# Graph attention layer on one core: the value product of a unit in two halves behind later scores, and operand stacks filled by halves of the tokens

## What is computed

```python
h = jnp.maximum(_layernorm(x), 0.0)            # x: (8, 1024, 256) f32
q = (h @ Wq + bq).reshape(b, n, 8, 32)         # k and v likewise
scores = jnp.einsum('bqhd,bkhd->bhqk', q, k) / sqrt(32)
scores = scores + (1.0 - adj)[None, None] * -1e9
attn = softmax(scores, axis=-1)
out = jnp.einsum('bhqk,bkhd->bqhd', attn, v).reshape(b, n, 256)
result = x + (out @ Wo + bo)
```

## Time and profile before

| | us |
|---|---|
| median of three runs (1271.64 to 1273.63) | 1272.16 |
| the profiled execution | 1269.52 |
| its span | 1267.7 |
| TensorE busy in the span | 1170.4 (92%) |
| DVE busy | 987.3 (78%) |
| ACT busy | 993.3 (78%) |
| POOL busy | 131.6 (10%) |

### The profile page before, as it was taken

How to read it: one execution, slowest core, us unless ns; L and a number is a source line. 1 busy time by engine, 2 the same in 40 slices (tenths; PEclk the granted TensorE clock), 3 DMA queues, 4 the chain that set the end, 5 groups by cost and what they waited for, 6 DMA issues and landing times.

```text
span 1267.7 us, 30114 instructions
## 1 busy us (share of the span) xinstructions
PE 1170.4 (92%) x10752; PEld 885.5 (70%) x10752; DVE 987.3 (78%) x1802; ACT 993.3 (78%) x1827; POOL 131.6 (10%) x235
## 2 busy tenths in 40 slices
PE   4799999999989999899999999999998999999897
PEld 4576776777767776676766777767776767777665
DVE  4697786977878877887878877888777978778775
ACT  2588886887878977788877878778877888778885
POOL 4002000020001101021010210002000020000001
PEclk9799999999999999999999999999999999999999
DMA  8442061511505134051431515225061320615001
GB/s 278 112 94 75 18 151 36 120 49 40 140 25 134 35 68 117 19 134 35 96 89 27 127 35 127 61 56 124 5 150 53 71 64 1 163 39 113 22 2 51
DMA packets 53470, 100.06 MB, mean 79 GB/s; under 512 B 10032, under 2 KB 35888, under 8 KB 53296
## 3 DMA queue, kind: packets, MB, share of 16 engines
q1 hardware_dynamic: 52720, 96.25, 30.3%
q0 software_dynamic: 576, 1.57, 0.5%
HBM read 22.28 MB, written 8.39 MB: 24 GB/s over the span
## 4 chain that ended last, share of the span: by engine, by line
PE 62%; ACT 21%; issue 8%; DVE 6%; SPq 1%; DMA 1%; ACTq 0%; POOL 0%; DVEq 0%; POOLq 0%
PE ps_turn L681 18%; PE ps_heads L737 18%; PE ps_scores L667 12%; ACT rows L420 11%; ACT turned_p L427 6%; PE ps_side L688 4%; PE ps_side L697 4%; PE ps_side L716 4%; DVE turned_p L515 3%; ACT turned_p L433 2%; SPq L248 1%; DVE rows L504 1%; ACT ht L445 1%; PE ps_turn L688 1%; DVE stats L539 1%
## 5 line engine op out<-in xcount | busy, mean ns | idle before, releaser
L504 DVE CUSTOM_DVE_ANT_0 rows<-ps_scores,mask 128x1024 f32<-128x1024 f32 x512 | 623.2, 1218 | 49.8 <-issue 29.8
L420 ACT ACTIVATE rows<-rows,row_min 128x1024 f32<-128x1024 f32 x512 | 591.5, 1155 | 31.3 <-DVE row_min L504 16.0
L681 PE MATMUL ps_turn<-ident_r,rows_raw 128*128 128x128 f32 x4096 | 499.6, 258 | 53.4 <-DVE turned_p L515 23.9
L681 PEld LDWEIGHTS ps_turn<-ident_r,rows_raw 128*128 128x128 f32 x4096 | 407.7, 141 | 189.2 <-issue 88.2
L427 ACT ACTIVATE turned_p<-ps_turn 128x512 f32<-128x512 f32 x512 | 307.5, 601 | 193.3 <-PE ps_turn L681 191.8
L515 DVE COPY turned_p<-ps_turn 128x512 f32<-128x512 f32 x384 | 263.3, 686 | 173.4 <-PE ps_turn L681 171.6
L667 PE MATMUL ps_scores<-k_stack,q_stack 128*128 128x512 f32 x1024 | 360.9, 434 | 12.3 <-DMA k_stack<-k_lo 12.3
L737 PE MATMUL ps_heads<-turned_p,v 128*32 128x256 f32 x4096 | 247.4, 382 | 11.3 <-ACT turned_p L427 10.8
L737 PEld LDWEIGHTS ps_heads<-turned_p,v 128*32 128x32 f32 x4096 | 120.1, 109 | 107.4 <-ACT turned_p L427 33.7
L667 PEld LDWEIGHTS ps_scores<-k_stack,q_stack 128*128 128x128 f32 x1024 | 153.9, 190 | 14.6 <-issue 7.7
L397 POOL COPY inv_wide<-row_inv 128x256 f32<-128x256 f32 x64 | 25.5, 398 | 1054.1 <-DVE row_inv L551 956.4
(11 more groups left out here) (55 smaller groups left out, 463.3 us busy)
## 6 DMA issues: line engine op xcount, KB each, us to landing
k_stack<-k_hi SPq DMA_DIRECT2D x128, 128.0 KB, 2.4
k_stack<-k_lo SPq DMA_DIRECT2D x128, 128.0 KB, 2.4
q_stack<-q_lo SPq DMA_DIRECT2D x124, 128.0 KB, 2.4
q_stack<-q_hi SPq DMA_DIRECT2D x120, 128.0 KB, 2.4
res<-in_x SPq DMA_DIRECT2D x32, 256.0 KB, 2.7
out<-res SPq DMA_DIRECT2D x32, 256.0 KB, 2.2
xn<-in_x SPq DMA_DIRECT2D x7, 1024.0 KB, 6.1
mask<-in_adj SPq DMA_DIRECT2D x1, 3584.0 KB, 14.8
```

Source lines behind the costliest of these rows:

```text
L420: nc.scalar.activation(rows[:, m % RING, :], rows[:, m % RING, :], ACT.Exp, bias=row_min[:, m % RING:m % RING + 1], scale=-1.0, accum_out= ...
L504: nc.vector.tensor_tensor_reduce(out=rows[:, m % RING, :], in0=ps_scores[m % 2][:], in1=mask[:, qt, :], scale=1.0, scalar=START_MIN, op0=A ...
L681: tr = nc.tensor.transpose(bank[:, k, :].bitcast(F32R), rows_raw[:, i % RING, kt * P:(kt + 1) * P], ident_r[:])
```

## The change

- The value product of a unit is split by key tiles. Half a runs behind the scores in slot 0 of the next unit, half b behind those in slot 3 (`PV_ROW`). The copies of half a and half b go to arrays of their own, turned_a and turned_b, with a place for each row (`place`), doubled for rows 0 (half a) and 0 to 3 (half b), so that the copies of the next unit's first rows don't overwrite what is still to be read. A matmul of it now reads two blocks of 128 columns.
- The row sums are inverted in slot 7 of their own unit, spread and transposed at the end of slot 7, and copied by ACT first in the next slot 0.
- ACT takes the high part, the ht copy and the copy of the inverses ahead of the exponential of its slot; before they stood behind it.
- `STEPS` puts the side work into other slots.
- q's and k's high and low parts hold half of the tokens only. After every qk step SP fills that half of the stack, by 16 transfers of 64 KB. So the high part of step 2 waits until the transfers of steps 0 and 1 have landed.
- Moments come one tile per slot, in slots 10 to 17 of phase 0. POOL normalises in unit 1 and not 2.
- bv isn't added to v any more: at the start TensorE multiplies bv by Wo and DVE adds it to bo.
- HEAD is 10.

```diff
-SIDE_STEPS = (
-    (("qk", 0, (1, 1, 2, 2)), ("o", 3, (3, 3, 4, 4)), ("qk", 1, (5, 5, 7, 7)), ("qk", 2, (9, 9, 11, 11)),
-     ("qk", 3, (13, 13, 14, 14)), ("v", 0, (17, 18, 19, 19)), ("v", 1, (21, 21, 22, 22)),
-     ("ht", 0, (26, 26, 26, 26)), ("ht", 1, (27, 27, 27, 27)), ("ht", 2, (29, 29, 29, 29)),
-     ("ht", 3, (30, 30, 30, 30))),
...
+PV_ROW = (0, 3)
+INV_ROW, NORM_ROW = 7, 4
+PLACES = (1 + UNIT_ROWS, PARTS + UNIT_ROWS)
...
+def place(half, u, r):
+
+    if half == 0:
+        return u % 2 if r == 0 else r + 1
+    return 2 * r + u % 2 if r < PARTS else PARTS + r
...
+STEPS = (
+    (("qk", 0, (1, 1, 2, 2)), ("o", 3, (5, 6, 7, 7)), ("qk", 1, (9, 9, 10, 10)), ("qk", 2, (12, 13, 14, 15)),
+     ("qk", 3, (17, 17, 18, 18)), ("v", 0, (20, 20, 21, 21)), ("v", 1, (23, 23, 25, 25)),
+     ("ht", 0, (27, 27, 27, 27)), ("ht", 1, (28, 28, 28, 28)), ("ht", 2, (29, 29, 29, 29)),
      ("ht", 3, (30, 30, 30, 30))),
...
+    (("qk", 0, (1, 1, 2, 2)), ("v", 0, (4, 4, 5, 5)), ("qk", 1, (6, 6, 7, 7)), ("v", 1, (9, 9, 10, 10)),
+     ("o", 0, (13, 14, 15, 15)), ("qk", 2, (17, 17, 18, 18)), ("qk", 3, (20, 21, 22, 22)),
+     ("o", 1, (25, 25, 26, 26)), ("o", 2, (29, 29, 30, 30))),
 )
```

SP:

```diff
+        def stack_step(eng, g, s):
+            n, cols = "qk"[s % 2], slice(s // 2 * BANK, (s // 2 + 1) * BANK)
+            dst, parts = {"q": q_stack, "k": k_stack}[n][g], parts_of(n, *hi, *lo)
+            for h in range(PARTS):
+                for r in range(PARTS):
+                    eng.dma_start(dst[r * HEAD_DIM:(r + 1) * HEAD_DIM, h, cols].bitcast(F32),
+                                  parts[r][h * HEAD_DIM:(h + 1) * HEAD_DIM, :].bitcast(F32)
+                                  ).then_inc(stacked[g][h], 16)
...
+            def stack(bg, g, s):
+                wait(lo_done, qk_step(bg, g, s) + 1)
+                stack_step(sp, g, s)
...
             def body(b, left):
-                stack(b, 1, row(b, 0, 0) + 1)
+                for s in range(1, QK_STEPS):
+                    stack(b, 1, s)
                 if left > 1:
...
                 if left > 0:
-                    stack(b + 1, 0, row(b, 1, 0))
...
+                    wait(scores_done, row(b, 1, 0) + 1)
+                    stack(b + 1, 0, 0)
+                    stack(b + 1, 0, 1)
+                store(b, 0, True)
+                if left > 0:
+                    stack(b + 1, 0, 2)
+                    stack(b + 1, 0, 3)
+                store(b, 1, True)
+                store(b, 2, left > 0)
+                if left > 0:
+                    first_step(b + 1)
+                store(b, 3, left > 0)
```

ACT's and DVE's slots:

```diff
             def slot(b, g, i, first, last):
+                r = i % UNIT_ROWS
+                kind, s, pieces = side_work(g, i - 1, first, last)
+                done = PIECES - 1 in pieces
+                if kind == "ht" and done:
+                    copy_ht(b + 1, s)
+                if kind == "qk" and done:
+                    nb, ng = next_phase(b, g)
+
+                    for h in range(PARTS):
+                        if s == 0:
+                            act.wait_ge(stacked[g][h], stack_count(g, b + 1))
+                        elif s == 2:
+                            act.wait_ge(stacked[ng][h], stack_count(ng, nb, 2))
+                    high_part(nb, ng, s, hi[s % 2][:])
+                if r == 0 and not (first and i == 0):
+                    copy_inv(unit(b, g, i // UNIT_ROWS) - 1)
                 m = ahead(g, i, EXP_AHEAD)
                 if not (last and m >= BATCH_ROWS):
                     exp(m, row(b, 0, m))
...
+                if r == INV_ROW:
+                    invert(b, g, u, first)
+                if r not in ACT_COPIES:
                     copy_b(b, g, i)
+                if r == NORM_ROW and not first:
+                    norm_heads(unit(b, g, u) - 1, *((g, u - 1) if u else (1 - g, UNITS - 1)))
+                if g == 0 and i in STATS and not last:
+                    moments(b + 1, STATS[i])
```

TensorE:

```diff
-                for kt in range(half * PARTS, (half + 1) * PARTS):
+                for kt in range(PARTS):
                     for h in range(PARTS):
-                        mm = nc.tensor.matmul(ps_heads[h * HEAD_DIM:(h + 1) * HEAD_DIM, 0:UNIT_Q],
-                                              v[g][:, kt, h * HEAD_DIM:(h + 1) * HEAD_DIM],
-                                              turned_p[:, h, kt, :], start=(kt == 0), stop=(kt == TILES - 1))
+                        p0, p1 = place(half, parity, h), place(half, parity, PARTS + h)
+                        mm = nc.tensor.matmul(ps_heads[h * HEAD_DIM:(h + 1) * HEAD_DIM, 0:UNIT_Q]
+                                              .rearrange("p (t n) -> p t n", n=P),
+                                              v[g][:, half * PARTS + kt, h * HEAD_DIM:(h + 1) * HEAD_DIM],
+                                              turned[half][:, p0:p1 + 1:p1 - p0, kt, :],
+                                              start=(half == 0 and kt == 0), stop=(half == 1 and kt == PARTS - 1))
...
             def slot(b, g, i, first, last):
-                n, u = row(b, g, i), i // UNIT_ROWS
-                for half in range(2):
-                    if i % UNIT_ROWS == 0 and not (first and i == 0):
-                        heads(n, unit(b, g, u), g if u else 1 - g, half)
-                    turn(b, g, i, half)
+                u, r = i // UNIT_ROWS, i % UNIT_ROWS
+                turn(b, g, i, 0)
+                turn(b, g, i, 1)
...
+                if r in PV_ROW and not (first and i < UNIT_ROWS):
+                    heads(unit(b, g, u) - 1, u + 1, g if u else 1 - g, PV_ROW.index(r))
...
+                if r == INV_ROW:
+                    turn_inv(b, g, u, first)
```

More of the change, by code:

```diff
@@ L262, in load_res, with wait @@
                              ).then_inc(res_in[u % 2], 16)
[L264 to L271 removed]
+            def wait(done, count):
+                count = held(sp, count)
+                sp.wait_ge(lo_done, QK_STEPS)
+                sp.wait_ge(done, count)
@@ new lines, in _, with spread, unit_work @@
+                stack_start(pool, start_stacked[h], h, "q", range(POOL_COPIES))
+            pool.wait_ge(bo_ready, 1)
+            def spread(b, g, u):
+                count = held(pool, unit(b, g, u) + 1)
+                own()
+                pool.wait_ge(inv_done, count)
+                pool.wait_ge(inv_turned, count)
+                pool.tensor_copy(inv_wide[:], row_inv[:].unsqueeze(2).to_broadcast([P, UNIT_ROWS, HEAD_DIM])
+                                 ).then_inc(inv_spread, 1)
+            def unit_work(b, g, u, last):
+                spread(b, g, u)
+                if (g, u) == (0, 0):
+                    add_bias(b, 0)
+                elif (g, u) == (0, 1) and not last:
+                    norm(b + 1)
+                elif (g, u) == (0, 2):
+                    add_bias(b, 1)
+                elif (g, u) == (1, 2):
+                    add_bias(b, 2)
+                elif (g, u) == (1, 3):
+                    add_bias(b, 3)
@@ L471, in slot @@
                     exp(m, row(b, 0, m))
-                kind, s, pieces = side_work(g, i - 1, first, last) or (None, 0, [])
-                done = PIECES - 1 in pieces
-                if i % UNIT_ROWS == INV_ROW + 1 and not (first and i < HEAD):
-                    copy_inv(unit(b, g, i // UNIT_ROWS))
-                if kind == "ht" and done:
-                    copy_ht(b + 1, s)
-                if kind == "qk" and done:
-                    if s == 0:
-                        for h in range(PARTS):
-                            act.wait_ge(stacked[g][h], stack_count(g, b + 1))
-                    high_part(*((b, 1) if g == 0 else (b + 1, 0)), s)
                 copy_a(b, g, i)
-                if i % UNIT_ROWS in ACT_COPIES:
+                if r in ACT_COPIES:
                     copy_b(b, g, i)
-            def tail():
-                copy_inv(BATCH * BATCH_UNITS)
-            slots(act, slot, tail)
+            slots(act, slot)
+            copy_inv(BATCH * BATCH_UNITS - 1)
         @block.vector
@@ L602, in slot @@
-                if kind == "o" and done:
-                    finish(b * UNITS + (0 if g == 0 else s + 1), s)
-                if g == 0 and not last:
-                    for t in STATS.get(i, ()):
-                        moments(b + 1, t)
-                u = i // UNIT_ROWS
-                if not (first and i < HEAD):
-                    pg, pu = (g, u - 1) if u else (1 - g, UNITS - 1)
-                    if i % UNIT_ROWS == 0:
-                        invert(unit(b, g, u), pu)
-                    if i % UNIT_ROWS == NORM_ROW:
-                        norm_heads(unit(b, g, u), pg, pu)
@@ L615, in slot @@
-                if i % UNIT_ROWS not in ACT_COPIES:
+                    mask_row(m, row(b, 0, m), m % ROWS // PARTS)
+                kind, s, pieces = side_work(g, i - 1, first, last)
+                if PIECES - 1 in pieces:
+                    nb, ng = next_phase(b, g)
+                    if kind == "qk":
```

(15 more changed lines are left out.)

320 lines of the change are left out of this document (148 added, 172 removed), and 3 rows, old and new, of the table SIDE_STEPS.

## The result

The changed kernel takes **1285.24 us** (median of 4 runs, 1284.10 to 1286.50); the kernel before took 1272.89 beside it. The ratio is **1.0093, with the interval 1.0072 to 1.0115**. I had forecast 1266: the change makes the kernel slower, by more than a measurement leaves open.

A forecast was written before the change was run, and what follows sets the result against it. TensorE, busy 92% of the span, was taken as the bound. Less work against slightly more waiting gave -4 us in eight batches, with -0.65 and -1.8 at the end -6.4 from the 1272.2 median: 1266 us, range 1238 to 1289.

The forecast's parts named there:

- Row 16 ... Wait 0.6: Phase 0, row 16: ACT's q_hi waits for the first half's stack transfers, landed 13.2 after row 11 began; 0.6 us per batch.
- My own upper bound: Phase 0, row 16: with 0.63 per issue and 2.4 for landing, the wait is 1.4 us.
- I am wrong if that q_hi waits 3 us: Sign of failure in slot 16 of phase 0, where ACT was expected to wait for a stack transfer under 1.5 us.
- DVE now has one tile's moments in each, 0.60: Phase 0, rows 12 to 15: moments add 0.60 per slot on DVE; rows 13 and 14 wait 0.25 and 0.67.
- the stack transfers become the bound: Rival, slot 16 of phase 0: landing 4.8 after issue, +2.6 per batch, 1287 us; chance 0.28 shared with dearer halves.
- the 0.15 of the estimate by the page: Stack transfers: by fixed cost plus bytes, a halved transfer lands some 0.15 us earlier, not in half the time.
- the argument on spreading: Value product: each unit has two slots of 3.19 for one of 5.19, high parts nearly all ahead of such slots.
- Rows 28 to 31 of phase 0: Four ht steps, ACT's copies longer than TensorE's work: about 9.3 us together, 3.0 of it waiting per batch.
- Phase 1's slot 23: Light row with q's or k's high part first on ACT: waits 1.5 us per batch.
- 10.4 against 9.9: Per batch in the loop: waits summed for the new order, 10.4 us, against 9.9 of removable waiting before.
- In the last phase 1 ... -1.8: Last phase 1, almost without side work: each unit has two slots behind slack for one, 4 x 0.45 = -1.8 us.
- Better spread: Rival: work spreads better than costed; 1250 us (chance 0.20), or 1225 if half of all waiting goes (0.12).

The follow-up runs named there:

- the experiment with the moments: Changed kernel with moments moved from slots 13 to 15 to slots 18 to 20 of phase 0, POOL normalising in unit 2: 1297.59 us, ratio 1.0210.
- eight fewer issues: Changed kernel with POOL, not SP, issuing heads 2 and 3 of k's first step for phase 1, so SP issues 8 of 16: 1262.85 us, ratio 0.9932.
- four orders around it: Changed kernel with v step first, ACT's exponential first, DVE's inversion first, and moments spread apart over slots 10 to 24 of phase 0: 1223.69 us, ratio 0.9624.

## Why the prediction was wrong

**The forecast of 1266 fails on two of its steps, whose waits were sized too small, and on one thing it did not price.**

*"Row 16 ... Wait 0.6"* is the step that failed. k's low part was done 3.2 after the turn of slot 11 began (375.79 to 379.03) where I took 2.0. An issue took 0.63, where I took 0.60; halving the bytes did nothing to it, had shown 0.63 with 128 KB. The last one landed 2.0 after its issue, and q_hi began 2.2 after it, as I had it. So 3.2+15x0.63+2.2 = 14.9 after slot 11 began, not 13.2, and ACT waited 2.5 to 4.0. (My own upper bound was added up wrong besides: with 0.63 and 2.4 the sum gives 1.25 and not 1.4.) "I am wrong if that q_hi waits 3 us", I had written: its mean is 24.9/8 = 3.1. In batches without a fall at slot 16 (0, 2, 4) TensorE lost only 0.8 by it (the slot is 3.95 to 4.00 there and 3.22 without the wait), because slots 13 and 14 were late as well and covered some of it; the experiment with the moments took that cover away, and so does batch 7, which has no moments.

*"DVE now has one tile's moments in each, 0.60"* was the second. The earlier trace rows show the pair inside a run of eight, where the second instruction of one overlaps the first of the next. Alone between a copy and a mask it takes 379.47 to 380.24 = **0.77**. DVE then has 2.51 per slot and not 2.34, and it came into slot 13 already behind by k's low part (0.74). Slots 13 and 14 took 3.10 and 2.51 for the 1.93 and 2.35 forecast, 1.3 us per batch.

**The granted clock** stood in no term, neither in the sum nor in a rival's price. Its falls cost about 14 us, for 1.5 before. Without them I estimate the changed kernel at 1273 (1285.2 less 12.4): the two steps above turned the forecast gain into none, and the clock made a loss of it. Three long issues, 3.6 us together, stood in no term either. The rival that I had named, *the stack transfers become the bound* at 1287, had the place, the direction and nearly the time (1285.2), and gave them a wrong cause: it asked for a landing of 4.8, while landing was 2.0 and the wait came from issue time and a late start. Its price of 2.6 per batch is not met by the wait, which costs TensorE 0.8 in batch 2; that its time is so near is luck, since falls of the clock make up the difference.

This is also where my use of the page "DMA: Bandwidth & Descriptors" of the Trainium skill stopped short. Its rule on small transfers speaks of those under 64 KB, measured from HBM, and gives 64 KB an efficiency of 32%. In this trace the cost that halving the bytes left as it was is the issue, 0.63 us for 64 KB as for 128 KB, 16 times in a row. Landing, which I worked out, went from 2.4 to 2.0, more than the 0.15 of the estimate by the page.

**What was right.** The halves are worth what the argument on spreading said, or more. A half product's slot is 3.22 (forecast 3.19). Rows 28 to 31 of phase 0 take 2.64+2.50+2.10+2.19 = 9.43 (forecast 9.3). Phase 1's slot 23 is 2.78 (1.32+1.5), slot 31 2.28 (1.32+0.13+0.9), the light slot 22 1.63 (1.32+0.4). The end is 0.62 shorter (1274.37 to 1284.0 against 1257.45 to 1267.7; forecast 0.65). The balance of waits, "10.4 against 9.9", came out 0.4 per batch above that in batch 2, the one without a fall, which is as long as those before: slots 13 and 14 cost 1.3 more, 15 and 16 0.3, and the loop's edge 1.2 less. At the edge TensorE idles 1.12 to 1.46, not the 2.42 that I had kept from the earlier trace rows. The timeline of TensorE at one edge, and at the last value product:

```profile
373.54 0.85 PE L700 MATMUL ps_turn<-ident_r,rows_raw 128*128 128x128 f32 x8 [1.17 <-issue]
...
1274.37 1.93 PE L760 MATMUL ps_heads<-turned_a,v 128*32 128x256 f32 x32 [0.56 <-ACT inv_wide L497]
```

*"In the last phase 1 ... -1.8"* did not come: the last batch is 4.8 longer, 4.2 of it in slot 16 (1.5 the fall, the rest the uncovered wait). With the wait gone ("eight fewer issues") it is 138.5 for 138.6 before, so nothing was won there either; no run shows why.

"Better spread", at 1225, had been the rival for what an order could win. The changed kernel isn't that, but 1224 is what it becomes when four orders around it are mended.

## What to carry to other kernels

When a step is cut into halves, count its issues and not its bytes: the queue that issues them one by one may become the bound, and the wait shows on an engine two steps away, behind whatever stands in front of the wait in order. Where a tuned order loses time in one slot, two engines can be late by the same amount, as in slot 23 here; test the two edits together before calling either useless. Where an edit leaves TensorE waiting in several slots in a row, put a price on the granted clock in one of the rivals. And compare the passes of a loop one by one in the trace: an average over them hid here that one pass had no fall and another lost 5.5 us.
